# One word cleared between gathers on GpSimd, in a graph network kernel

## What is computed

```python
# L0, attention, 2 heads of 128
e = jax.nn.leaky_relu(xl[src] + xr[dst], NEG_SLOPE)
alpha = _segment_softmax(jnp.einsum('ehd,hd->eh', e, att), dst, n)
out = jax.ops.segment_sum(xl[src] * alpha[..., None], dst, num_segments=n)
...
# L2, GINE, three layers
for l in range(W1.shape[0]):
    e = edge_attr @ W_lin[l] + b_lin[l]
    msg = jax.nn.relu(x[src] + e)
    agg = jax.ops.segment_sum(msg, dst, num_segments=n)
    h = jax.nn.relu((x + agg) @ W1[l] + b1[l]) @ W2[l] + b2[l]
    x = relu(batchnorm(h))
```

## Time and profile before

| | |
|---|---|
| median of three runs | 5072.95 us (5072.32 to 5081.31) |
| the profiled execution, its own time | 5085.52 us |
| its span, first to last instruction | 5083.7 us |
| mean granted TensorE clock | 0.784 of full speed |
| busy: TensorE, VectorE, ScalarE, GpSimd | 70%, 52%, 32%, 50% |
| gathers: GINE, first attention, second attention, edge MLP | 1176, 488, 488, 416 |

### The profile page before, as it was taken

One profiled execution on the slowest core, in us unless ns is written; L12 is line 12 of the kernel. 1 busy time (PEld: TensorE's weight loads), 2 busy tenths in 40 slices (PEclk: granted clock), 3 DMA queues, 4 the chain that ended last, 5 costly groups with the idle time before them and its releaser, 6 DMA issues. The chain is left out here.

```text
span 5083.7 us, 91413 instructions
## 1 busy us (share of the span) xinstructions
PE 3545.7 (70%) x20792; PEld 2661.7 (52%) x20793; DVE 2651.7 (52%) x6184; ACT 1604.4 (32%) x3137; POOL 2542.1 (50%) x2650
## 2 busy tenths in 40 slices
PE   6999999777777634554635555455555699999997
PEld 3666666544444424443424444244444578787874
DVE  6777777745555532332322232323323677777775
ACT  3566666544444421111201111111112433333334
POOL 3555555356666655555365555355553344444440
PEclk7999999889999955555655555655556899999998
DMA  3333333222222211111111111111111333333330
GB/s 104 94 92 93 92 93 93 73 57 65 66 67 67 65 46 49 53 51 51 46 51 52 51 53 52 47 51 51 52 52 35 94 96 100 95 100 95 101 94 16
DMA packets 293250, 349.78 MB, mean 69 GB/s; under 512 B 63536, under 2 KB 236755, under 8 KB 292915
## 3 DMA queue, kind: packets, MB, share of 16 engines
q0 software_dynamic: 98528, 229.12, 16.0%
q1 hardware_dynamic: 140481, 92.05, 6.5%
q10 hardware_dynamic: 54162, 27.77, 1.9%
HBM read 332.61 MB, written 16.07 MB: 69 GB/s over the span
## 5 line engine op out<-in xcount | busy, mean ns | idle before, releaser
L986 POOL DMA_INDIRECT gath<-source_rows_narrow,gine_idx x1176 | 1127.1, 958 | 925.7 <-SPq L967 488.5
L1000 PE MATMUL psum<-gine_lin,ea 32*128 32x128 f32 x2928 | 290.2, 486 | 1034.9 <-DVE vs L1034 969.9
L1064 ACT ACTIVATE pm<-vs 128x512 f32<-128x512 f32 x366 | 230.5, 630 | 1809.1 <-DVE vs L1034 1548.6
L1000 PEld LDWEIGHTS psum<-gine_lin,ea 32*128 32x128 f32 x2928 | 185.1, 299 | 1137.1 <-DVE vs L1034 910.4
L1140 POOL DMA_INDIRECT gath<-source_rows,idx_all x416 | 428.9, 1031 | 636.6 <-DVE vs L1261 452.2
L1009 PE MATMUL psum<-hot,pm 128*128 128x128 f32 x2928 | 730.0, 428 | 8.5 <-ACT pm L1064 8.3
L760 POOL DMA_INDIRECT gath<-source_rows,idx_all x488 | 469.0, 961 | 433.1 <-PE psum L807 318.2
L1034 DVE TENSOR_TENSOR vs<-psum,gath 128x512 f32<-128x512 f32 x366 | 253.2, 692 | 820.6 <-remote 518.3
L1009 PEld LDWEIGHTS psum<-hot,pm 128*128 128x128 f32 x2928 | 626.9, 316 | 91.2 <-ACT pm L1064 53.9
L760 POOL DMA_INDIRECT gath<-source_rows_narrow,idx_all x488 | 462.0, 947 | 329.5 <-remote 140.3
L790 PE MATMUL psum<-lk,att_b 128*128 128x512 f32 x732 | 403.7, 638 | 123.1 <-issue 67.9
(11 more groups left out here) (238 smaller groups left out, 5631.0 us busy)
## 6 DMA issues: line engine op xcount, KB each, us to landing
rel<-rel_rows SPq DMA_DIRECT2D x244, 128.0 KB
ea<-in_edge_attr_tiles SPq DMA_DIRECT2D x416, 64.0 KB
ea<-in_edge_attr ACTq DMA_DIRECT2D x366, 64.0 KB
gath<-source_rows_narrow,gine_idx POOLq DMA_INDIRECT x1176
gath<-source_rows,idx_all POOLq DMA_INDIRECT x904
rel<-quad_rel_rows SPq DMA_DIRECT2D x104, 128.0 KB
gath<-source_rows_narrow,idx_all POOLq DMA_INDIRECT x488
source_rows<-ACC SPq DMA_DIRECT2D x12, 512.0 KB, 2.9
```

What stands on the lines that cost most here:

```text
L986: pool.indirect_dma_start(out=ring[:, g % RING, j, :], out_offset=None, in_=table1, in_offset=bass.IndirectOffsetOnAxis(ap=gine_idx[:, g, ...
L1000: last = e.matmul(E[:, j, :], ea[rows, s, :], gine_lin[rows, layer, :], start=True, stop=True)
```

## The change

After each gather of the first attention (`heads == 2`) and of the three GINE layers GpSimd writes 0.0 to one 4-byte word in partition 0 of a tile that the stage does not use: word `4 i + j` of `ea_all` in the attention, word `4 g + j` of `lk` in the GINE layers. The memset waits for nothing and signals nothing. The second attention and the edge MLP keep their gathers as they are.

```diff
                 @block.gpsimd
                 def _(pool):
+                    spare = ea_all[:, :, :].rearrange("p a n -> p (a n)")
                     for i in range(ITEMS):
                         wait(pool, o_ready, before_h + heads * (i - 3))
                         for j in range(SUBS):
                             pool.indirect_dma_start(
                                 out=gath[:, i % 4, j, 0:width], out_offset=None, in_=dram,
                                 in_offset=bass.IndirectOffsetOnAxis(ap=idx_all[:, i, j:j + 1], axis=0)).then_inc(gathered[i % 4], 16)
+                            if heads == 2:
+                                pool.memset(spare[0:1, SUBS * i + j:SUBS * i + j + 1], 0.0)
...
                 @block.gpsimd
                 def _(pool):
                     pool.wait_ge(gine_idx_in, 16)
+                    spare = lk[:, :, :].rearrange("p a n -> p (a n)")
                     for g in range(GROUPS):
                         if g >= RING:
                             pool.wait_ge(gi_free, layer * GROUPS + g - RING + 1)
                         for j in range(SUBS):
                             pool.indirect_dma_start(
                                 out=ring[:, g % RING, j, :], out_offset=None, in_=table1,
                                 in_offset=bass.IndirectOffsetOnAxis(ap=gine_idx[:, g, j:j + 1], axis=0)).then_inc(gi_gath[g % RING], 16)
+                            pool.memset(spare[0:1, SUBS * g + j:SUBS * g + j + 1], 0.0)
```

## The result

The changed kernel takes 5089.64 us (median of 20 runs, 5072.06 to 5101.13), the kernel before 5073.28 beside it (20 runs, 5063.9 to 5084.19): a ratio of 1.003, 95% interval 1.0022 to 1.0038. It is 16 us slower, where 4830 was forecast. The profiled execution has a span of 5092.6 us, against 5083.7 before.

The account below looks back on a forecast made before the run. GINE layers were taken to wait for TensorE signals held behind runs of gathers. Saving 81 us a layer, 243 in three, with nothing from the first attention, gave 5073 - 243 = 4830 us; range 4745 to 5090.

Parts of the forecast that it names:

- What bounds the kernel: GINE layers, 40% of the span, wait for TensorE signals held during long rows of gathers; first attention bound by matmuls.
- The rate and the threshold: GINE gathers are worked off at 1.40 us each but issued every 1.25; stretching the step by over 0.15 ends the backlog.
- The run of 44: 44 unbroken gathers at a GINE layer's start; TensorE's signals said to let go after 61.94 us.
- the run of 12: Twelve unbroken GINE gathers; signals let go after 17.21 us, 3.20 us behind the start of the last gather.
- rival (b): GINE holds follow the run's end, not the rate, so memsets cost 235 us: 5308; 0.17 with its smaller form.
- x: Time by which a memset moves GpSimd's next gather: taken as 0.20 us, 0.10 duration plus 0.10 handover; bounds 0 to 0.38.
- The lower end of the bounds: Memset handed over in 0.03 us and run inside the 0.30 us before every gather, so it moves the next by 0.
- Rival (a): Memset too short or hidden, moving the next gather under 0.15 us: no change, 5073 within 5 us; chance 0.25.
- Below it the hold ends at the same moment as before: GINE layers: if a memset moves the next gather under 0.15 us, backlog still grows and the time does not move.
- The first attention: TensorE idles only 26 of 832 us; memsets put an item's last gather back 0.8 us, 3.5 to spare: no change.
- VectorE and TensorE can follow 5.8 us a group: GINE layers without holds: TensorE, the busiest other engine, needs 3.4 us per group against 5.8 for four gathers.
- The sum for a release in the middle: GINE layer 572 us of gathers plus 22 for landing and remaining holds: 594 against 675, 243 us less in three.

Follow-up runs that it names:

- 320 words: Against the kernel before, a 320-word memset after each GINE gather, with a wait for the previous memset and a semaphore: 4824.27 us, 0.9499.
- the long memset: Against the kernel before, a memset after each GINE gather, with wait and semaphore, of 512 words: 4985.46 us, 0.9817; of 1024 words: 5554.05 us, 1.0936.
- 256 words: Against the kernel before, a 256-word memset after each GINE gather, with a wait for the previous memset and a semaphore: 4967.57 us, 0.9796.
- 192 words: Against the kernel before, a 192-word memset after each GINE gather, with a wait for the previous memset and a semaphore: 5007.02 us, 0.9867.
- 288 words: Against the kernel before, a 288-word memset after each GINE gather, with a wait for the previous memset and a semaphore: 4883.46 us, 0.9606.
- the empty instructions: Against the kernel before, no memset but two empty instructions after each GINE gather, each adding one to an unawaited semaphore: 5137.81 us, 1.0113.

## Why the prediction was wrong

**What bounds the kernel** was read rightly. The GINE layers wait for held signals: with most of the holds gone their three layers fall from 2025 to 1774 us (320 words, "remote" 344 us, not 992) while TensorE, VectorE and ScalarE do the same work (TensorE busy 994.60 us in the three windows with 320 words, 996.68 before). The forecast failed at the price of the memset, not at the waits.

**The rate and the threshold** stand, with one size off. The backlog per gather was put at 1.40 us, from runs begun from empty. The run of 44 in the earlier trace rows was read loosely: 61.94 us is its last release and not its first. An earlier one, L1043, is

```profile
1894.04 0.29 DVE L1043 TENSOR_TENSOR ACC<-ACC,psum 128x128 f32 x1 [20.97 <-remote]
```

which is 3.08 us behind the start of the last gather, near the 3.20 of the run of 12. So what the prediction held against rival (b), that this distance is not constant, was weaker than it says; what decides against (b) is the long memset. The last release stands in all three layers (61.94, 61.98 and 61.96 us). The L1034 taken for the landing was timed from 1840.85, but the fourth gather starts at 1840.98; nothing hangs on that.

The threshold measured is 1.44 to 1.47: with 256 words, whose step of 1.413 is above 1.40, GpSimd still stops 56 times. With 192 words the last signals came free 5.88 us after the start of a run of 4 (median of 38) and 74.29 after that of the run of 52, (74.29 - 5.88) / 48 = 1.43 us per further gather, at a step of 1.36. So the rate where memsets stand between is a little lower than in the earlier trace rows, but that does not bring it to 1.44. Nearer than that it can't be read from runs: with 256 and 288 words the holds lengthen with the step itself. Why a step just above the rate is not yet enough stays open; that some gathers take 1.1 to 1.5 us and not 0.95 (98 of 1176 with 288 words, where the mean step is 1.468; 62 in the kernel before) may have a part in it. x would have to be 0.19 to 0.22, not 0.15. The 0.20 that I took for x lies inside that, so even had it been true, the 4830 was not certain: the kernels on either side of it took 4883 (x = 0.19) and 4824 us (x = 0.22).

**The price x** is the step that failed. The prediction weighed the 0.30 us before a gather and held that it "seems to begin only when the instruction before is done", from the DMA of L617, which starts 0.30 us behind a cast. It does not: in the profile the memset of 0.09 us and the 0.16 us behind it fit into the 0.30 that run from the end of the gather. The 0.30 behind that cast is a wait for the cast, as its row says, and of another kind of DMA; I carried it over to a gather that waits for nothing. Behind a memset a gather comes after 0.16. The lower end of the bounds (x = 0, inside the 0.30) was in the text, with the earlier trace rows for it, and got 0.25; the prediction chose against it on the row of the cast alone.

Rival (a) is what happened: the memset is hidden, x is under 0.15, and the time moves little. The Trainium skill (GPSIMD Engine Reference, section Instruction dispatch) says that consecutive Pool instructions are no barrier between the cores; by that rule the prediction had x near 0 and nearly the right time, but by a way that these runs don't show. No memset is shown to start inside a gather (2101.74 + 0.94 = 2102.68, the memset starts at 2102.69); by the profile, whose spans of GpSimd are rough, it hides in the gap behind the gather, not beside it.

**The 5073 within 5 us of rival (a)** was still 16 us short, because I held that an instruction that moves no gather moves nothing. "Below it the hold ends at the same moment as before" does not hold for signals that are given in the middle of a run: more of them get out one gather later. That this makes the 16 us is read from the counts above and from the empty instructions, which raise both; why it happens stays open.

**The first attention** was right: the stage is 3 us longer in a trace whose like vary by 9, and memsets there alone give 1.0002. So was that VectorE and TensorE can follow 5.8 us a group: with 320 words four gathers and memsets make 6.0 and GpSimd never waits for a slot. **The sum for a release in the middle** holds but for its 22 us: 392 x (1.26 + x) + 22 with the mean step of 1.494 that 320 words show (x = 0.23) makes 608; the layers took 589 to 594, since no hold stops GpSimd any more and only the 8 us behind the last gather apply (594). **Rival (b)** fell with the long memset.

Of the signs named for the profile after, the step over 1.40 us, "remote" under 300 us and the waits for a slot under 150 us were all absent (1.25, 1052.5 and 474.1 us), and the step under 1.40 was named as the sign of (a). "No run of 44" alone held, and misled: the layers now open with a run of 30, which is no release.

## What to carry to other kernels

Where many gathers go out back to back from GpSimd and another engine's waits end in "remote", compare the step between gathers with the time per gather at which the signals come free; to stretch the step a little past it was faster here than to gather as fast as the queue takes them. A short instruction does not stretch it: the gap behind a gather swallows it. Size the filler by a few lengths on either side of the threshold, since 0.03 us of step moved the time by 59 us here. Leave it out where the engines are not held, and where four stretched gathers take as long as an item does now: in the second attention it ended the holds and won nothing.

## What the runs showed that I had not expected

- A memset of 0.09 us behind a gather does not move the next gather; from 0.25 us on a gather starts 0.16 us behind the memset, not 0.30. By these two the free length would end at 0.30 - 0.16 = 0.14 us, an estimate: no length between was run.
- A memset of one partition on GpSimd takes 0.087 us plus 0.83 ns a word.
- Instructions without any effect on the step of the gathers, two per gather, made the kernel 1.1% slower, and with them more signals came out 1.43 us later. The same two only behind the last gather of a group, ahead of the wait for a slot, cost nothing (1.0007).
- TensorE's last held signal of a run came free at 1.40 us per gather where gathers stand alone, 1.43 with 192 words between, and only a step between 1.436 and 1.466 us rid the layers of the stops.
